# Macaron block on one core: the order of loads, turned maxima, square roots, projections and turning where attention meets the second FFN

## The reference

```
x = x + 0.5 * ffn(layernorm(x))
x = x + attn(layernorm(x))
x = x + 0.5 * ffn(layernorm(x))
```

## Time and profile before

| quantity | value |
|---|---|
| median of 3 runs | 1023.23 us (1022.47 to 1023.43) |
| the profiled execution | 1024.88 us |
| its span, first to last instruction | 1023.2 us |
| PE busy | 966.8 us, 94% |
| DVE busy | 838.1 us, 82% |
| ACT busy | 513.6 us, 50% |
| POOL busy | 261.8 us, 26% |
| mean granted TensorE clock | 0.975 |

### The profile page before, as it was taken

How to read it: one execution, slowest core, us unless ns; L and a number is a source line. 1 busy time by engine, 2 the same in 40 slices (tenths; PEclk the granted TensorE clock), 3 DMA queues, 4 the chain that set the end, 5 groups by cost and what they waited for, 6 DMA issues and landing times.

```text
span 1023.2 us, 18097 instructions
## 1 busy us (share of the span) xinstructions
PE 966.8 (94%) x5602; PEld 575.6 (56%) x5602; DVE 838.1 (82%) x2476; ACT 513.6 (50%) x1027; POOL 261.8 (26%) x289
## 2 busy tenths in 40 slices
PE   6899999999888699999999999999887999999997
PEld 5678887888655233333333333333343777777776
DVE  6677776777675899999999999999756888888775
ACT  4225433442322277777777777777776333232210
POOL 1012212221420421221222222222333443434211
PEclk9999999999996599999999999999998999999999
DMA  6201101112113412222222323322320112110001
GB/s 220 86 1 62 63 0 62 62 46 78 62 49 78 123 29 69 72 70 71 71 72 75 76 76 75 76 75 75 85 64 8 47 62 63 62 53 20 10 21 41
DMA packets 55059, 64.27 MB, mean 63 GB/s; under 512 B 13777, under 2 KB 37313, under 8 KB 54977
## 3 DMA queue, kind: packets, MB, share of 16 engines
q1 hardware_dynamic: 54384, 62.47, 21.4%
q10 hardware_dynamic: 592, 0.80, 0.2%
HBM read 41.30 MB, written 21.23 MB: 61 GB/s over the span
## 4 chain that ended last, share of the span: by engine, by line
PE 83%; DVE 7%; ACT 3%; issue 3%; DMA 2%; SPq 1%; POOL 1%; DVEq 0%; POOLq 0%; ACTq 0%
PE bank L353 39%; PE bank L1312 13%; PE bank L1485 13%; PE bank L1469 12%; PE bank L345 2%; PE bank L792 2%; DMA c_rec<-att_rec 1%; ACT b_probs L1448 1%; DMA v_all<-L_ffn_w_experts 1%; DVE bank L1339 1%; DVE c_acc L989 1%; PE bank L743 1%; DVE b_neg L1343 1%; DVE a_acc L989 1%; DVE a_st L308 1%
## 5 line engine op out<-in xcount | busy, mean ns | idle before, releaser
L1448 ACT ACTIVATE b_probs<-bank 128x512 f32<-128x512 f32 (+1 forms) x608 | 302.4, 587 | 108.5 <-PE bank L1469 108.3
L1312 PE MATMUL bank<-b_ks,b_qs 96*128 96x512 bf16 (+3 forms) x768 | 226.8, 338 | 18.4 <-DVE b_neg L1339 6.2
L1339 DVE CUSTOM_DVE_ANT_0 bank<-bank,b_below 128x384 f32<-128x384 f32 (+3 forms) x512 | 234.9, 516 | 2.4 <-PE bank L1312 0.8
L1469 PE MATMUL bank<-b_qs,b_ks 99*128 99x512 bf16 (+3 forms) x768 | 215.3, 331 | 4.7 <-ACT b_probs L1448 4.6
L353 PE MATMUL bank<-we,a_xt 128*128 128x512 f32 x768 | 190.7, 402 | 2.0 <-DVE a_acc L989 2.0
L353 PE MATMUL bank<-we,c_xt 128*128 128x512 f32 x768 | 187.7, 399 | 1.1 <-DVE c_acc L989 1.1
L1422 POOL TENSOR_SCALAR_AFFINE_SELECT b_probs<-b_probs 128x512 f32<-128x512 f32 x128 | 81.5, 642 | 339.1 <-ACT b_probs L1448 339.1
L1343 DVE TENSOR_REDUCE b_neg<-bank 128x1 f32<-128x512 f32 x256 | 160.6, 679 | 3.6 <-PE bank L1312 2.1
L353 PEld LDWEIGHTS bank<-we,a_xt 128*128 128x128 f32 x768 | 143.2, 191 | 30.8 <-DVE a_acc L989 1.7
L353 PEld LDWEIGHTS bank<-we,c_xt 128*128 128x128 f32 x768 | 141.9, 189 | 32.5 <-DVE c_acc L989 1.6
L1485 PE MATMUL bank<-b_probs,b_vs 128*32 128x512 f32 (+3 forms) x1536 | 154.5, 496 | 0.9 <-POOL b_probs L1422 0.9
(11 more groups left out here) (135 smaller groups left out, 887.8 us busy)
## 6 DMA issues: line engine op xcount, KB each, us to landing
b_qs<-q_parts SPq DMA_DIRECT2D x96, 128.0 KB, 3.0
b_ks<-k_parts SPq DMA_DIRECT2D x96, 128.0 KB, 3.1
q_parts<-a_part SPq DMA_DIRECT2D x16, 384.0 KB, 2.7
k_parts<-a_part SPq DMA_DIRECT2D x16, 384.0 KB, 2.7
att_num<-b_oev SPq DMA_DIRECT2D x64, 64.0 KB, 2.2
c_num<-att_num SPq DMA_DIRECT2D x8, 512.0 KB
c_rec<-att_rec SPq DMA_DIRECT2D x16, 256.0 KB
out<-xs SPq DMA_DIRECT2D x8, 512.0 KB, 3.1
```

What stands on the lines that cost most here:

```text
L1312: last = nc.tensor.matmul(ms[bank][:, a * width:(a + 1) * width], qs[g.u][0:ROWS, c, i * P:(i + 1) * P], ks[g.u][0:ROWS, c, lo:lo + width] ...
L1339: last = dve.tensor_tensor_reduce(part, part, below[:, CH - width:CH], -1.0, 3.0e38, ALU.add, ALU.min, dst[:, a, :])
L1448: act.activation(probs[b % 4][:, heads[0]:heads[0] + hp, 0:width], es[exp_bank(g, unit)][:, 0:hp * width].rearrange("p (h w) -> p h w", w= ...
L1469: last = nc.tensor.matmul(es[exp_bank(g, unit)][:, a * width:(a + 1) * width], ks[g.u][:, c, j * P:(j + 1) * P], qs[g.u][:, c, first_q:fir ...
```

## The change

Six calls move to another block or entry; nothing is added and nothing removed.

```diff
     # ACT
-                if (early, block) == (0, 6):
+                if (early, block) == (0, 4):
                     std_of(act, 0, mv, std, q.normed_aggr, q.std_done)
                     std_of(act, 1, mv3, std3, q.aggr3, q.std3)
                 if (early, block) == (0, 7):
                     split_hi(0, 0)
-                if (early, block) == (0, 8):
+                if (early, block) == (0, 9):
                     logits_out(0)
     # PE
-                if (early, block) == (0, 3):
+                if (early, block) == (0, 2):
                     project(1, 1, (0,))
                     project(1, 1, (1,))
-                if (early, block) == (0, 6):
+                if (early, block) == (0, 7):
                     turn(0)
-                if (early, block) == (0, 8):
+                if (early, block) == (0, 9):
                     router(0, 0)
-                if (early, block) == (0, 9):
+                if (early, block) == (0, 10):
                     turn_logits(0)
     # DVE
-                if (early, block) == (1, 23):
+                if (early, block) == (1, 24):
                     dve.wait_ge(a.v_copied, at(NG))
                     attended(0, 0, 0)
                     attended(1, 1, 0)
     # POOL, in every group but the last
-                if b == 4 and exists(g + 1):
+                if b == 2 and exists(g + 1):
                     pool.wait_ge(summed, at(nkb * g.n))
                     copy_values(pool, g + 1)
```

## The result

| kernel | median us | range of its runs |
|---|---|---|
| before | 1022.65 | 1021.96 to 1023.43 (6) |
| changed | 1027.38 | 1026.84 to 1028.33 (6) |

The ratio is 1.0045 (95% interval 1.0035 to 1.0056): **4.6 us slower** (3.6 to 5.7), outside the stated range. The profiled execution took 1028.33 us, its span 1026.6.

The account below looks back on a forecast made before the run. PE work bounds the kernel, so only moving chunk 2's projection (789.76) counts: -1.7 in group 14, +1.1 in group 15, net -0.6, taken as -0.4 for the clock, giving 1022.8 us; range 1020.6 to 1024.9.

Parts of the forecast that it names:

- Group 14, -1.7: DVE in group 14: reading the turned maxima before `attended` removes PE's wait for `b_turned`, so group 15 starts 1.7 us earlier.
- Projection of chunk 1: PE, group 15: its 16 matmuls go ahead of block 3's scores, ready 2 us before ACT wants them; cost and gain zero.
- Roots after block 4, turn after block 7: Group 15: ACT waits about 2.9 us, PE stands 6.2 us before block 5's last unit, the 4.52 us `turn(0)` wait goes.
- the sum: Group 14 gives -1.7 us, group 15 becomes 1.1 longer: net -0.6, or -0.4 with a little for the clock.
- Router, logits and their turning one block later: End of group 15: mask 3.1 us after the turned logits, `turn_mask` waits some 0.4 us beside the last copy-out.
- The clock: PE in group 15: recovers as quickly as before; +1.9 us if half clock held to about 777, -0.3 if never fallen.
- the slower rival: Rival A: half clock stays through blocks 5 to 7 of group 15, +1.9 us; chance 0.17.
- POOL's copy: POOL, 15 groups: copy of the values at block 2 costs zero, with 1.1 us spare before block 3's product.
- A: PE from 769.3 in group 15: half clock stays through blocks 5 to 7, +1.9, net +1.3, 1024.5 us; chance 0.17.
- B: Group 15: DVE's chunk 1 chain ready when ACT comes, blocks 5 to 8 unheld; -3.5, 1019.7 us; chance 0.12, whole or half.
- C: POOL's copy holds back block 3's product, 0.3 x 15 = +4.5, 1027.3 us; chance 0.04.
- D: Group 14: first projection at 745.15 finds another wait (reciprocals' DMA), -1.7 shrinks, sum +0.7, 1023.9 us; chance 0.12.

## Why the prediction was wrong, point by point

- **Group 14, -1.7:** right for that pair of profiles (-1.96), wrong as a term of the median. It took a DMA landing of one execution (745.42) for the rule; where it landed at 743.3 a kernel without this edit had the same stretch A, and PE waited for `b_turned` in only two of five profiles without it. Alone the edit gave -0.8 (-1.7 to +0.1).
- **Projection of chunk 1:** not run alone; in the profile block 3's scores lay ready before ACT came to them, as forecast.
- **Roots after block 4, turn after block 7:** every wait was sized right (2.89 and 6.24 us), and the half clock of the group was over by 773, as in the sum. `turn(0)` began at 776.88, which is 777.3 on the scale of the profile before, forecast 777.2. But group 15 became longer by 2.20 to the last product, forecast +1.1. Of the 1.1 between them 0.3 is no loss, only what group 14 gained over its 1.7. The other 0.8 comes behind the turn: 0.3 by the end of the router, 0.4 by the turning of the logits, 0.8 by the last product. 0.2 of it is POOL's last select (0.84 us beside DVE's `ranks`, 0.63 in the profile before); the rest I did not resolve. The sum also priced the clock inside group 15 too low: it had -0.3 if the clock never fell, and filling the gap made stretch B 1.24 shorter. That the hold alone is free I had not seen.
- **Router, logits and their turning one block later: the step that failed.** It said that the mask comes 3.1 us after the turned logits and that `turn_mask` waits 0.4 us beside the copy-out. That 3.1 was read where the mask's write met only the end of one of POOL's selects (0.40 us, against 0.21 alone). One block later it starts in step with POOL's `add_bias(2)` and lasts until that is done, 2.39 us; PE waits 1.87 us for it instead of 0.4 beside the copy-out. The profile before had the pattern in plain sight, in rows that I read past: the mask ends with the select, and `c_ln` on four numbers a partition takes 1.46 us, up to the end of POOL's `shift_x`.

```profile
786.69 0.63 POOL L1422 TENSOR_SCALAR_AFFINE_SELECT b_probs<-b_probs 128x512 f32<-128x512 f32 x1 [1.26 <-ACT b_probs L1448]
790.70 2.42 POOL L490 TENSOR_TENSOR c_xb<-xs,beta 128x1024 f32<-128x1024 f32 x1
791.68 1.46 DVE L321 SCALAR_TENSOR_TENSOR c_ln<-c_mv,c_ln 128x4 f32<-128x4 f32 x1
```

POOL waiting for the mask, all else as changed, brought the write to 0.21 us and took off about half of the loss, in an execution that also kept the clock; late router and collision alone, in the kernel before, cost +1.9 us (1.1 to 2.9).

- **The clock, a term put at nothing:** I priced it only inside group 15 (the slower rival, +1.9). It fell again at 790, behind group 15, and cost 2.96 us there, the largest row of the table. I had treated as the one place, though PE works thinly over the last two products too (1.67 of 4 us in the changed kernel). That place is on the edge: of 12 profiles of either order without fillers there, 8 had the half clock in chunk 2's projection (5.38 to 6.65 us), 4 had not. All five in which PE waited the 1.9 us for the mask had it; of the seven without that wait, three had it. So the fall goes with the wait, and comes without it too. Why the two profiles of the changed kernel paid the longer price (6.65 and 6.62) and the other six 5.38 is open; only these two have both the unfilled wait for the mask and the unfilled gap of the hold.
- **POOL's copy:** free, as forecast (+0.1).
- **The rivals:** A named the half clock, but at the wrong place. That B and C did not happen was right, and in this pair D did not either. None had two engines slowing each other.

The rule that I had weighed, that activity releases the throttle (the Trainium skill, TensorE: Matmul & The Clock Gate, Part 1), holds in these traces: fillers alone kept 1.00 in six kernels, each where they stood. The collision has its rule there too: the Trainium skill (GPSIMD Engine Reference, 1. Specifications) says that POOL's SBUF interfaces are shared with VectorE, with contention for some of its instructions. The trace agrees: the mask's write took 0.21 us alone and 2.39 beside POOL's `add_bias(2)`, until that ended.

## What to carry to other kernels

Before moving a small VectorE instruction on a critical chain, look at what GpSimd runs at its new place: its price can be that of GpSimd's whole instruction. A wait of TensorE can cost twice where the engine is thinly used already, once itself and once at half clock in the dense work behind it; matmuls that nobody reads, placed in waits that are there anyway, gave 1.8 us (0.9 to 2.7) in the kernel before. And a wait on a DMA that one profile shows is one draw: compare a second profile before it becomes a term of the sum.

## What the runs showed of the hardware that I had not expected

- Very small DVE instructions lasted until the POOL instruction beside them ended: the mask's write took 2.38 to 2.41 us in seven profiles, always ending with `add_bias` (2.34 to 2.36 us); 0.40 or 0.41 in nine, ending with a select; and 0.21 in the one where POOL did nothing beside it; a 32x128 subtraction (line 1331) 2.28 us beside `add_bias(0)` in the changed kernel, 0.28 in the one before. Not all of them do: the reduction to `c_rank` took 0.42 us beside a select in both profiles, and the copy of `b_turned` from PSUM 0.27 us beside one in the profile before, 0.28 without.
- The same order gave both clocks at the same place: the projection of chunk 2 took 3.69 us in the first profile of the kernel before, 5.38 with only POOL's copy moved.
- With the same loads, the second `attended`, which waits for the second reciprocals, began at 736.5 to 745.4 us, or 5.6 to 9.6 us behind the turning of the maxima on PE.
